# A strided convolution with three products for two outputs, and segments of 25 times instead of 26

## The chip, the cores and the metric

The kernel runs on one core of a Trainium2 chip. The metric is the device time in microseconds (us) of one execution; lower is better. The engines are called by name: TensorE (PE in the profile, its weight loads PEld), VectorE (DVE), ScalarE (ACT), GpSimd (POOL) and SyncE (SP).

## The reference, cut to what matters

An audio tower: seven strided convolutions, each followed by a layer norm over its 128 channels and a GELU, then a projection to 192 features, one attention block and a mixture of nine experts. The change touches the convolutions.

```python
CONVS = [(128, 10, 5)] + [(128, 3, 2)] * 4 + [(128, 2, 2)] * 2    # channels, taps, stride
h = x[:, None, :]                                                # x: 64 rows of 4000 samples
for w, g, b, s in zip(conv_ws, ln_gs, ln_bs, strides):
    h = _conv1d(h, w, s)
    h = jnp.swapaxes(h, -2, -1)
    h = _fp32_layernorm(h, g, b)
    h = jnp.swapaxes(h, -2, -1)
    h = jax.nn.gelu(h, approximate=False)
```

Layer 0 gives 799 times for each row, layer 1 gives 399, then 199, 99, 49, 24 and 12. All is float32.

## The kernel before

The 64 rows are worked in NT = 8 groups of 8. In layers 0 and 1 each row is cut into SEG = 16 segments of LEN1 = 26 layer-1 times, so 8 x 16 = 128 segments lie on the 128 partitions, and the kernel computes 416 layer-1 times for the 399 that are wanted. Layer 0 is computed in LOCALS = 54 local times in blocks of twelve ("quads" q = 0 to 4, the last one shorter), which ScalarE's GELU writes into a ring of four blocks.

The work is written out by hand as a list of slots, SLOTS = HEAD (groups 0 and 1) + BODY for the groups 2 to 6 (16 slots each) + LAST (group 7) + DRAIN. A slot is (chunk, jobs, prep). A chunk (l, g, k) is one PSUM bank of convolution outputs of layer l, group g: up to four blocks of 128 channels for up to 128 positions; CUTS gives the blocks of each chunk. BODY is written relative to g: its slot 0 is (1, g, 0), slot 8 is (1, g, 2), slot 10 is (1, g, 4), slot 11 is (1, g, 3). Each engine walks all slots in the same order and takes its part:

- TensorE: `conv` of slot k's chunk, then `turn` (transposes) of the chunk of slot k - 2, then the jobs, then the token steps (attention and router of a group that is through).
- ScalarE: `square` of slot k, then `gelu` of slot k - 2, then its jobs ("l0": GELU of layer 0).
- VectorE: `norm` of slot k - 1, then `group` (the sum of squares) of slot k, then its jobs ("raw", "z", "xt") and "xs" parts.
- GpSimd: `group` of slot k, a power that turns the sums into factors (L603), then the "pow" parts of layer 0's factors (L597; 12 or 10 columns each), then token steps such as `power_2` (L608 and L610).

So one chunk goes: conv, square (L1378), sum (L1089), power (L603), norm (L1098, which multiplies out of PSUM into `xh`), turn (L771), gelu (L1397). Three PSUM banks hold convolutions, one (`tr`) the transposes, and two hold jobs in turn behind the head: before TensorE starts a job, `room` waits until the job two places ahead of it in the list has been taken out by ScalarE or VectorE.

In layer 1, `conv` multiplies each local time (stationary) with the taps (moving). Outputs j and j + 1 share the local time between them, and so that one is multiplied with two taps at once, 256 columns wide (L751); a chunk of four outputs is 12 blocks of 128 columns. The taps lie in `wt`, W2s holds the experts' second weights, all nine loaded when group 3's samples are.

## Time and profile before

| | us |
|---|---|
| median of 3 runs | 583.17 |
| lowest, highest | 581.24, 583.61 |
| the profiled execution | 581.46 |
| its span, first to last instruction | 579.7 |
| TensorE busy | 549.2 (95%) |
| VectorE, ScalarE, GpSimd busy | 318.1, 316.5, 264.4 |

Busy time is what an engine spent in instructions, and 1.8 us of the profiled execution lie outside its span. float32 products appear as two records each, so "x24" is 12 products. Durations of overlapping instructions of one engine can add up to more than the stretch they fill; the distance between two starts is then the better figure.

### The profile page before, as it was taken

The numbers are of one execution on the slowest core, as the hardware profiler recorded it, in microseconds if no ns is written. First come the engines' busy times: TensorE is split into PE (matmuls) and PEld (weight loads), VectorE is DVE, ScalarE is ACT, GpSimd is POOL, SyncE is SP. The second block draws the span as 40 slices with busy tenths as digits, with TensorE's granted clock in tenths as the row PEclk, the third lists the DMA queues.
The fourth block names the chain that finished last, engine by engine and source line by source line (L and its number), as shares of the span: only waits on it lengthen the run. The fifth ranks groups of instructions, "written<-read, shape, count | busy, mean of one in ns | idle before, by whom it ended". The sixth has DMA issues, their size and how long they took to land.

```text
span 579.7 us, 11208 instructions
## 1 busy us (share of the span) xinstructions
PE 549.2 (95%) x4191; PEld 517.1 (89%) x4191; DVE 318.1 (55%) x751; ACT 316.5 (55%) x499; POOL 264.4 (46%) x297
## 2 busy tenths in 40 slices
PE   6899999999999999999999999999999996899995
PEld 5697999989999999999999989989898975789995
DVE  4666465565567666856574666554654443612231
ACT  1566666747665675558455846574554423344440
POOL 4674394693248426732754294324423030133443
PEclk9999999999999999999999999999999996799999
DMA  6191000792000000000000000000000069051110
GB/s 178 42 329 41 1 1 11 182 211 43 2 1 11 2 6 1 1 7 1 2 0 7 1 1 2 6 1 1 6 2 5 3 174 223 19 158 38 49 38 11
DMA packets 17519, 26.35 MB, mean 45 GB/s; under 512 B 2172, under 2 KB 13397, under 8 KB 17467
## 3 DMA queue, kind: packets, MB, share of 16 engines
q1 hardware_dynamic: 14155, 15.85, 10.1%
q0 software_dynamic: 3296, 9.78, 7.2%
q8 instruction: 35, 0.57, 0.4%
q14 instruction: 17, 0.14, 0.1%
q10 hardware_dynamic: 16, 0.00, 0.0%
HBM read 17.13 MB, written 9.18 MB: 45 GB/s over the span
## 4 chain that ended last, share of the span: by engine, by line
PE 82%; POOL 7%; DVE 4%; ACT 4%; issue 2%; DMA 1%; SPq 1%; POOLq 0%; DVEq 0%; ACTq 0%
PE ps L759 23%; PE ps L751 9%; PE ps L771 7%; PE ps L748 7%; POOL rstd L597 5%; PE ps L1015 4%; PE ps L824 4%; PE ps L1004 3%; PE ps L1003 3%; PE ps L845 3%; PE ps L815 2%; PE ps L886 2%; PE ps L749 2%; PE ps L753 2%; PE ps L906 2%
## 5 line engine op out<-in xcount | busy, mean ns | idle before, releaser
L603 POOL TENSOR_TENSOR rstd<-ssum,neghalf 128x4 f32<-128x4 f32 (+7 forms) x128 | 116.9, 914 | 194.3 <-DVE ssum L1089 194.1
L759 PE MATMUL ps<-wt,wide 128*128 128x128 f32 (+2 forms) x1248 | 151.0, 275 | 4.6 <-ACT wide L1397 4.6
L1378 ACT ACTIVATE work<-ps 128x512 f32<-128x512 f32 (+7 forms) x128 | 67.2, 525 | 161.3 <-PE ps L753 81.9
L759 PEld LDWEIGHTS ps<-wt,wide 128*128 128x128 f32 (+2 forms) x1248 | 144.2, 184 | 7.5 <-issue 6.2
L1089 DVE TENSOR_REDUCE ssum<-work 128x4 f32<-128x516 f32 (+7 forms) x128 | 76.0, 594 | 69.7 <-ACT work L1378 69.2
L1098 DVE TENSOR_TENSOR work<-ps,rstd 128x512 f32<-128x512 f32 (+7 forms) x128 | 76.2, 595 | 68.5 <-POOL rstd L603 67.8
L1397 ACT ACTIVATE wide<-ps,lncol 128x512 f32<-128x512 f32 (+6 forms) x120 | 109.5, 912 | 5.7 <-PE ps L771 5.3
L597 POOL TENSOR_TENSOR rstd<-var,half 128x10 f32<-128x10 f32 (+2 forms) x39 | 82.9, 2133 | 9.0 <-DVE var L1056 8.4
L1408 ACT ACTIVATE h<-ps,lncol 128x512 f32<-128x512 f32 (+1 forms) x120 | 82.0, 730 | 2.4 <-PE ps L824 2.4
L751 PE MATMUL ps<-wt,h 128*128 128x256 f32 x304 | 74.9, 380 | 0.0
L771 PE MATMUL ps<-ident,work 128*128 128x128 f32 (+2 forms) x424 | 66.2, 270 | 0.5 <-DVE work L1098 0.2
L751 PEld LDWEIGHTS ps<-wt,h 128*128 128x128 f32 x304 | 53.5, 191 | 4.9
L748 PE MATMUL ps<-wt,h 128*128 128x128 f32 x416 | 56.0, 276 | 0.2 <-ACT h L1408 0.2
L748 PEld LDWEIGHTS ps<-wt,h 128*128 128x128 f32 x416 | 52.5, 192 | 1.4 <-issue 0.5
L771 PEld LDWEIGHTS ps<-ident,work 128*128 128x128 f32 (+2 forms) x424 | 49.7, 141 | 2.1 <-issue 1.0
L824 PE MATMUL ps<-cols,w0t 120*128 120x512 f32 (+1 forms) x120 | 43.5, 425 | 2.5 <-ACT h L1408 1.6
L1467 ACT ACTIVATE work<-ps 128x768 f32<-128x768 f32 x13 | 10.5, 810 | 35.7 <-PE ps L1004 35.7
L608 POOL TENSOR_TENSOR veps<-mv,eps 96x1 f32<-96x1 f32 x24 | 5.5, 228 | 49.3 <-DVE mv L1108 49.2
L1015 PE MATMUL ps<-W2s,work 128*128 x156 | 27.6, 327 | 0.1
L707 POOL DMA_INDIRECT out_dram<-xnat,idt x13 | 13.1, 1006 | 30.8 <-DVE xnat L1335 30.2
L1077 DVE CAST cols<-ps 120x512 fp32r<-120x512 f32 (+1 forms) x40 | 25.1, 629 | 1.9 <-PE ps L815 1.8
L1318 DVE COPY xst<-ps 96x256 f32<-96x256 f32 x13 | 5.5, 421 | 37.3 <-issue 26.9
(227 smaller groups left out, 833.6 us busy)
## 6 DMA issues: line engine op xcount, KB each, us to landing
sorted_tokens<-zero POOLq DMA_DIRECT2D x1, 5886.5 KB, 33.9
W2s<-in_L_ffn_W_dram SPq DMA_DIRECT2D x9, 576.0 KB, 8.7
wide<-in_L_ffn_W_dram SPq DMA_DIRECT2D x8, 576.0 KB
cols<-sorted_tokens SPq DMA_DIRECT2D x13, 96.5 KB, 2.0
xnat<-in_x_dram SPq DMA_DIRECT2D x7, 135.0 KB
wt<-in_L_ffn_b_dram SPq DMA_DIRECT2D x1, 864.0 KB, 4.4
wide<-in_L_tok_conv_w_dram SPq DMA_DIRECT2D x4, 192.0 KB, 3.4
common_sums<-acc POOLq DMA_DIRECT2D x1, 579.0 KB, 5.3
```

The source lines that it names most:

```text
L597: gp.tensor_tensor(rstd0[:, lo:hi], var0[:, lo:hi], half0[:, lo:hi], ALU.pow).then_inc(s_pow, 1)
L603: gp.tensor_tensor(rstd[0:rows, idx, 0:count], ssum[0:rows, idx, 0:count], neghalf[0:rows, 0:count], ALU.pow).then_inc(rstd_done, 1)
L748: nc.tensor.matmul(y[:, j * C:(j + 1) * C], local(2 * (lo + j) + 1), wt[:, 0, :], start=(j == 0), stop=False)
L751: nc.tensor.matmul(y[:, (j - 1) * C:(j + 1) * C], local(2 * (lo + j)), wt[:, 1:3, :].rearrange("p t c -> p (t c)"), start=False, stop=False)
L759: last = nc.tensor.matmul(y[0:rows, j * C:(j + 1) * C], h[l - 1][g % 2][:, at:at + rows], wt[:, TAP0[l] + tap, :], start=(tap == 0), stop= ...
L771: last = nc.tensor.transpose(tr[:, j * rows:(j + 1) * rows], xh[0:rows, n % 2, j * C:(j + 1) * C], ident[0:rows, 0:rows])
L824: nc.tensor.matmul(o[:, 0:w], w0t[:, j, :], xcol[q % 2][0:12 * K0, 0:w], start=True, stop=True).then_inc(j_done, 1)
L1089: nc.vector.reduce_sum(ssum[0:rows, n % 4, 0:count], sq[0:rows, n % 2, 0:count, :], axis=X).then_inc(ssum_done, 1)
L1098: nc.vector.tensor_tensor(xh[0:rows, n % 2, 0:w].rearrange("p (j c) -> p j c", c=C), ybank(n)[0:rows, 0:w].rearrange("p (j c) -> p j c", c=C),
L1378: nc.scalar.activation(sq[0:rows, n % 2, 0:CUTS[l][k], 0:C], ybank(n)[0:rows, 0:w].rearrange("p (j c) -> p j c", c=C), ACT.Square).then_in ...
L1397: nc.scalar.activation(dst, src, ACT.Gelu, bias=lncol[:, 8 + l:9 + l], scale=lncol[:, l:l + 1]).then_inc(act_done, 1)
L1408: nc.scalar.activation(dst, src, ACT.Gelu, bias=lncol[:, 8:9], scale=lncol[:, 0:1]).then_inc(j_act, 1)
```

## The change

Two outputs of layer 1, y0 = A x0 + B x1 + C x2 and y1 = A x2 + B x3 + C x4, are computed from m = (A + C) x2 as y0 = m + A (x0 - x2) + B x1 and y1 = m + B x3 + C (x4 - x2). For a chunk of four outputs that gives:

- GpSimd makes the four differences with two subtractions of 128x256 (`differences`, prep "df", at the start of a slot's part); it waits for layer 0's ring and for the end of the chunk that last used the buffer. Once, it makes A + C (`wt[:, NTAP]`).
- TensorE does two products for the middle into a job bank (`job_mid`, ahead of the chunk's other products, with `room`'s wait), four with B, waits for the differences, and does four with A or C: ten of 128 columns.
- ScalarE copies the middle out of PSUM (`job_mid`), VectorE adds it to the chunk (`add_mid`) into `ysum` in SBUF, ahead of its `norm` of the slot before; `square` and `norm` read `ysum`. In such slots ScalarE's order is middle, `gelu` of slot k - 2, `square`.
- Segments have 25 times (400 layer-1 times), LOCALS is 51, the last chunk of layer 1 has one output instead of two, layer 0's last quad one triple instead of two, and ROWS_OF shrinks for the layers 2 to 5. As 25 is odd, a layer-1 `gelu` is now two instructions of half the size.
- The new buffers lie in the room of three experts' second weights, which are loaded when the last shared chunk of group 7 is normed instead of at group 3.
- The jobs, "pow" parts and token steps are placed in other slots; LAST keeps its chunks and jobs.

```diff
-LEN1 = 26
-ROWS_OF = [P, P, P, 120, 104, 104, 104]
-LOCALS = 2 * LEN1 + 2
+LEN1 = 25
+ROWS_OF = [P, P, 124, 116, 100, 100, 104]
+LOCALS = 2 * LEN1 + 1
-CUTS = [None, (4, 4, 4, 4, 4, 4, 2), (4, 3, 3, 3), (4, 3), (4,), (2,), (1,)]
+CUTS = [None, (4, 4, 4, 4, 4, 4, 1), (4, 3, 3, 3), (4, 3), (4,), (2,), (1,)]
...
+    ((2, -1, 2), [], []),
+    ((2, -1, 1), [('raw', 1), ('xt', 0, 3)], []),
+    ((2, -1, 0), [], []),
+    ((5, -2, 0), [('l0', 0, 2, 2), ('l0', 0, 3, 0)], []),
+    ((2, -1, 3), [('l0', 0, 3, 2), ('z', 1, 0)], [('pow', 1, 0), ('pow', 1, 1), ('df', 0, 2)]),
+    ((1, 0, 2), [('l0', 0, 3, 1), ('z', 1, 1)], []),
+    ((6, -2, 0), [('xt', 0, 4)], [('pow', 1, 2), ('pow', 1, 3), ('df', 0, 4)]),
+    ((1, 0, 4), [('l0', 0, 4, 0), ('l0', 0, 4, 1), ('l0', 0, 4, 2)], [('pow', 1, 4), ('xs', 1, 0), ('df', 0, 3)]),
+    ((1, 0, 3), [('xt', 1, 0)], []),
+    ((3, -1, 1), [('l0', 1, 0, 1), ('l0', 1, 0, 0)], []),
+    ((3, -1, 0), [('xt', 1, 1), ('l0', 1, 0, 2)], [('df', 0, 5), ('xs', 1, 1)]),
+    ((1, 0, 5), [('l0', 1, 1, 0), ('l0', 1, 1, 1)], []),
+    ((1, 0, 6), [('l0', 1, 1, 2)], [('df', 1, 0)]),
...
+            def differences(g, k):
+                i, lo, count = DIFF[(g, k)], first_block(1, k), CUTS[1][k]
+                quads = range(2 * lo // BLK, 2 * (lo + count) // BLK + 1)
+                gp.wait_ge(j_act, max(ACT_TO[job_at(g, q) + 1] for q in quads))
+                if i >= 2:
+                    gp.wait_ge(conv_done, NUMBER[(1, *DIFFS[i - 2])] + 1)
+                for p in range(count // 2):
+                    at = 2 * lo + 4 * p
+                    before, mid, behind = (local(g, at + d) for d in (0, 2, 4))
+                    out, step = dif[:, i % 2, 2 * p:2 * p + 2, :], behind.offset - before.offset
+                    if step > 0:
+                        ends = bass.AP(before.tensor, before.offset, [before.ap[0], [step, 2], [1, P]])
+                        last = gp.tensor_tensor(out, ends, mid.unsqueeze(1).to_broadcast([P, 2, P]), ALU.subtract)
...
             for k, (chunk, _, prep) in enumerate(SLOTS):
+                for what, g, i in prep:
+                    if what == "df":
+                        differences(g, i)
                 if chunk is not None:
                     group(NUMBER[chunk])
...
+            def job_mid(job):
+                _, g, k = job
+                o = room(job)
+                pe.wait_ge(s_mid, 1)
+                for p in range(CUTS[1][k] // 2):
+                    last = nc.tensor.matmul(o[:, p * C:(p + 1) * C], local(g, 2 * first_block(1, k) + 4 * p + 2), wt[:, NTAP, :],
+                                            start=True, stop=True)
+                last.then_inc(j_done, 1)
...
                 if l == 1:
+                    job_mid(("mid", g, k))
                     for j in range(count):
-                        nc.tensor.matmul(y[:, j * C:(j + 1) * C], local(2 * (lo + j) + 1), wt[:, 0, :], start=(j == 0), stop=False)
-                    nc.tensor.matmul(y[:, 0:C], local(2 * lo), wt[:, 2, :], start=False, stop=False)
-                    for j in range(1, count):
-                        nc.tensor.matmul(y[:, (j - 1) * C:(j + 1) * C], local(2 * (lo + j)),
-                                         wt[:, 1:3, :].rearrange("p t c -> p (t c)"), start=False, stop=False)
-                    nc.tensor.matmul(y[:, (count - 1) * C:count * C], local(2 * (lo + count)), wt[:, 1, :],
-                                     start=False, stop=True).then_inc(conv_done, 1)
+                        nc.tensor.matmul(y[:, j * C:(j + 1) * C], local(g, 2 * (lo + j) + 1), wt[:, 0, :], start=(j == 0), stop=False)
+                    pe.wait_ge(s_diff, DIFF[(g, k)] + 1)
+                    for j in range(count):
+                        last = nc.tensor.matmul(y[:, j * C:(j + 1) * C], dif[:, DIFF[(g, k)] % 2, j, :],
+                                                wt[:, 1 if j % 2 else 2, :], start=False, stop=(j == count - 1))
+                    last.then_inc(conv_done, 1)
...
+            def add_mid(n):
...
+                ve.wait_ge(j_act, ACT_TO[JOB[("mid", g, k)] + 1])
+                ve.wait_ge(conv_done, n + 1)
+                nc.vector.tensor_tensor(made(n)[:, 0:w].rearrange("p (h d c) -> p h d c", h=half, d=2),
+                                        ybank(n)[:, 0:w].rearrange("p (h d c) -> p h d c", h=half, d=2),
...
             for k, (chunk, jobs, _) in enumerate(SLOTS):
-                if chunk is not None:
+                if shares_taps(chunk):
+                    job_mid(NUMBER[chunk])
+                elif chunk is not None:
                     square(NUMBER[chunk])
                 if k >= LAG and ORDER[k - LAG] is not None:
                     gelu(NUMBER[ORDER[k - LAG]])
+                if shares_taps(chunk):
+                    square(NUMBER[chunk])
```

## Rows read from the trace of the kernel before

**Rows 1.** The page: busy time of each engine, shares of the chain that ended last.

```profile
PE 549.2 (95%) x4191; PEld 517.1 (89%) x4191; DVE 318.1 (55%) x751; ACT 316.5 (55%) x499; POOL 264.4 (46%) x297
...
PE 82%; POOL 7%; DVE 4%; ACT 4%; issue 2%; DMA 1%; SPq 1%; POOLq 0%; DVEq 0%; ACTq 0%
```

**Rows 2.** Stretches: length, busy time by engine, granted clock, DMA share, GB/s.

```profile
294.00:348.00 54.00, 53.36 (x431) 50.87 (x430) 34.93 (x79) 33.99 (x55) 27.69 (x28) 1.00 0.01 2
```

**Rows 3.** Chain that ended last, one group: start us, us, what.

```profile
309.57 1.30 PE ps L751 x6
311.47 2.63 PE ps L759 x24
314.10 0.44 PE ps L771 x4
...
319.23 0.46 PE ps L824 x2
...
329.26 0.97 PE ps L906 x12
```

**Rows 4.** TensorE in order of time, one group: start us, us, idle before.

```profile
277.76 0.60 PE L771 MATMUL ps<-ident,work 128*128 128x128 f32 x4
...
283.22 0.66 PE L759 MATMUL ps<-wt,wide 128*104 128x128 f32 x4 [0.63 <-ACT wide L1397]
...
290.54 0.38 PE L753 MATMUL ps<-wt,h 128*128 128x128 f32 x2
...
332.15 0.60 PE L771 MATMUL ps<-ident,work 128*128 128x128 f32 x4
```

**Rows 5.** GpSimd in order of time, same group.

```profile
279.12 0.85 POOL L603 TENSOR_TENSOR rstd<-ssum,neghalf 128x3 f32<-128x3 f32 x1 [2.77 <-DVE ssum L1089]
280.08 4.50 POOL L597 TENSOR_TENSOR rstd<-var,half 128x12 f32<-128x12 f32 x2
...
285.52 1.95 POOL L597 TENSOR_TENSOR rstd<-var,half 128x10 f32<-128x10 f32 x1
287.44 0.55 POOL L603 TENSOR_TENSOR rstd<-ssum,neghalf 104x1 f32<-104x1 f32 x1
287.96 1.96 POOL L597 TENSOR_TENSOR rstd<-var,half 128x10 f32<-128x10 f32 x1
...
290.16 0.84 POOL L610 TENSOR_TENSOR rs<-veps,neghalf 96x1 f32<-96x1 f32 x1
290.97 1.01 POOL L603 TENSOR_TENSOR rstd<-ssum,neghalf 128x4 f32<-128x4 f32 x1
```

**Rows 6.** GpSimd's groups by form: busy us, mean ns.

```profile
L608 POOL TENSOR_TENSOR veps<-mv,eps 96x1 f32<-96x1 f32 x24 | 5.5, 228 | 49.3 <-DVE mv L1108 49.2
...
L573 POOL TENSOR_TENSOR centre<-centre,ident 128x128 f32<-128x128 f32 x1 | 0.5, 453 | 0.1
```

**Rows 7.** ScalarE in order of time, same group.

```profile
311.12 0.60 ACT L1378 ACTIVATE work<-ps 128x512 f32<-128x512 f32 x1 [1.77 <-PE ps L753]
311.62 0.80 ACT L1397 ACTIVATE wide<-ps,lncol 128x256 f32<-128x256 f32 x1
312.20 0.37 ACT L1420 COPY act<-ps 96x192 f32<-96x192 f32 x1
```

**Rows 8.** VectorE in order of time, same group.

```profile
310.36 0.69 DVE L1098 TENSOR_TENSOR work<-ps,rstd 128x512 f32<-128x512 f32 x1 [0.24 <-POOL rstd L603]
```

**Rows 9.** ScalarE's groups by form: busy us, mean ns.

```profile
L1408 ACT ACTIVATE h<-ps,lncol 128x256 f32<-128x256 f32 x24 | 12.4, 556 | 0.0
```

**Rows 10.** Start of the kernel: GpSimd in order of time.

```profile
12.08 10.22 POOL L597 TENSOR_TENSOR rstd<-var,half 128x12 f32<-128x12 f32 x4 [6.49 <-DVE var L1056]
```

**Rows 11.** Start of the kernel: TensorE in order of time.

```profile
21.07 1.05 PE L748 MATMUL ps<-wt,h 128*128 128x128 f32 x8
...
23.70 0.60 PE L815 MATMUL ps<-ident,xhl 128*120 128x128 f32 x4
```

**Rows 12.** DMA issues: KB each, median us to landing.

```profile
W2s<-in_L_ffn_W_dram SPq DMA_DIRECT2D x9, 576.0 KB, 8.7
```

More of the change, by code:

```diff
@@ L150 @@
 LAST = [
-    ((1, 7, 0), [], []),
+    ((1, 7, 0), [], [('df', 7, 1)]),
     ((1, 7, 1), [], []),
@@ L208, with shares_taps @@
 SLOTS = HEAD + [row for g in range(2, NT - 1) for row in body(g)] + LAST + DRAIN
+def shares_taps(chunk):
+    return chunk is not None and chunk[0] == 1 and CUTS[1][chunk[2]] > 1
+SLOTS = [(c, ([("mid", c[1], c[2])] if shares_taps(c) else []) + jobs, prep) for c, jobs, prep in SLOTS]
 AFTER = [('down', 6), ('up', 3, 0), ('up', 3, 1), ('up', 3, 2), ('up', 3, 3), ('up', 3, 4), ('up', 3, 5), ('down', 7)]
@@ L215 @@
 NG = len(CHUNKS)
+FIRST = [n for n, c in enumerate(CHUNKS) if shares_taps(c)]
+PAIRED = {n: i for i, n in enumerate(FIRST)}
+DIFFS = [p[1:] for row in SLOTS for p in row[2] if p[0] == "df"]
+DIFF = {d: i for i, d in enumerate(DIFFS)}
 JOBS = [j for row in SLOTS for j in row[1]] + AFTER
@@ L218 @@
 assert len(JOB) == len(JOBS)
-ON_ACT = ("l0", "up")
-HEAD_JOBS = sum(len(row[1]) for row in HEAD)
+ON_ACT = ("l0", "up", "mid")
+HEAD_JOBS = sum(len(row[1]) for row in SLOTS[:len(HEAD)])
 BANK = [4 + n % 4 if n < HEAD_JOBS else 4 + n % 2 for n in range(len(JOBS))]
@@ L420, in ybank, with made, local @@
             return ps[:, n % 3, :]
+        def made(n):
+            return ysum[:, PAIRED[n] % 2, :] if n in PAIRED else ybank(n)
+        def local(g, at):
+            return ring[:, (QUADS * g + at // BLK) % RING, at % BLK, :]
         def jbank(j):
@@ L597, in power_first @@
                 gp.tensor_tensor(rstd0[:, lo:hi], var0[:, lo:hi], half0[:, lo:hi], ALU.pow).then_inc(s_pow, 1)
+            def differences(g, k):
[11 more added lines that the diff above has]
+                        last = gp.tensor_tensor(out, ends, mid.unsqueeze(1).to_broadcast([P, 2, P]), ALU.subtract)
+                    else:
+                        gp.tensor_tensor(out[:, 0, :], before, mid, ALU.subtract)
+                        last = gp.tensor_tensor(out[:, 1, :], behind, mid, ALU.subtract)
+                last.then_inc(s_diff, 1)
             def group(n):
@@ L975, in _ @@
                 for job in jobs:
-                    if k > 2:
+                    if k > 2 and job[0] != "mid":
                         WORK[job[0]](job)
@@ L1261, in _ @@
                 for job in jobs:
-                    if job[0] not in ON_ACT and k > 2:
+                    if job[0] not in ON_ACT and job[0] != "mid" and k > 2:
                         WORK[job[0]](job)
@@ L1449, in _ @@
                     gelu(NUMBER[ORDER[k - LAG]])
+                if shares_taps(chunk):
+                    square(NUMBER[chunk])
                 for job in jobs:
-                    if job[0] in ON_ACT and k > 2:
+                    if job[0] in ON_ACT and job[0] != "mid" and k > 2:
                         WORK[job[0]](job)
```

132 lines of the change are left out of this document (97 added, 35 removed), and 51 rows, old and new, of tables (BODY, HEAD).

## The prediction

> **What bounds the kernel.** Start with the page [rows 1]: TensorE is busy 95% of the span, and 82% of the chain that ended last runs through it. The stretches say whether that holds in the middle, where the five bodies of 16 slots lie: in one of 54 us TensorE is busy 53.36, VectorE 34.93, ScalarE 33.99, GpSimd 27.69, at the full clock [rows 2]. One body takes 332.15 - 277.76 = 54.39 us, read between two starts of the same transposes, those behind slot 7's convolution [rows 4]. I call that moment E7. So the kernel goes at the rate of TensorE's queue, and every column taken from it is time, as long as what TensorE waits for is there in time. The other engines have 20 to 27 us of air in a body, but they walk in order and in bursts, and that is where this change has to be read.
>
> **What the change takes from TensorE.** The chain gives the pitch: 12 products of 128 columns in 2.63 us, so 0.22 each, and three of 256 in 1.30, so 0.433 each: a wide one is worth two, and time goes by columns [rows 3]. A shared chunk falls from 12 blocks to 10: 2 x 0.22 = 0.43 us. Six of them in a group give 2.6. The chunk with one output instead of two saves three blocks, 0.66, and a transpose, 0.11 (four take 0.44 [rows 3]). Layer 0's last quad is one triple shorter: 3 x 0.06 and one transpose, 0.3 in all; two layer-0 products of 512 columns take 0.46 [rows 3]. The narrower transposes of the layers 2 to 5 give less than 0.1. In all 3.7 us a group, 8 groups, about 29 us: the most that the change can give. Besides, slot 9 waited 0.63 us for the GELU before it in every body [rows 4]; more work now stands between the two, so that this goes: 0.6 more a body. Without any new wait a body would take about 50.1.
>
> **What it adds elsewhere.** On VectorE one add of 512 elements, like the norm at 0.69 [rows 8]: 4.1 a body. On ScalarE a copy out of PSUM, taken as the 128x192 copy at 0.37 [rows 7], and a second instruction for each GELU: a layer-1 GELU of 256 elements lets the next start 0.58 us after it [rows 7], so a pair costs 1.16. On GpSimd two subtractions a chunk. The trace has no such instruction. The two nearest are 228 ns for one column and 453 for 128 [rows 6]; a line through them gives 0.68 us at 256 columns. Bounds: as cheap as the one of 128 columns, 0.45, and twice that, 0.9. Call a chunk's differences D: 1.4 taken, 0.9 to 1.8. All three engines stay below 80% of a body, so none becomes the bound by its sum.
>
> The Trainium skill (GPSIMD Engine Reference, on elementwise work side by side with VectorE) has 4497 ns for an add of 2048 float32 elements and about 2.6 cycles an element at 1.2 GHz, and says to keep such work on VectorE. An estimate from it is 0.56 us and a dispatch for 256 columns; the slope between our two rows, 1.8 ns an element, agrees roughly. By its rate D would be 1.4 to 1.5, and the sum would stay.
>
> **Where it waits: slots 7 to 11.** GpSimd's order there is: power of chunk 7, "pow" 12 and 12 columns, power of chunk 8, differences of chunk (1, g, 4), power of chunk 9, "pow" 10 and 10, `power_2`, differences of chunk (1, g, 3). All of it but the two differences is in today's trace in nearly the same order: it starts at 279.12, which is E7 + 1.36, and ends where the next power starts, at 290.97, with no gap [rows 5]. That is 11.85 us, and with both differences the last of them are there at E7 + 1.36 + 11.85 + 2 x 1.4 = E7 + 16.0. Only then can slot 11 do its last four products, 0.9, and end at E7 + 16.9. Today slot 11's convolution ends at about 290.76 (last products start at 290.54 [rows 4]), E7 + 13.0; nothing on TensorE waited for GpSimd, because the power of a chunk is wanted only two slots later, while differences made in slot 10 are wanted in slot 11. TensorE itself would be there at about E7 + 13.2: three chunks less (-1.3) and the wait of 0.63 gone, but the attention's value products and two layer-0 products moved in (+0.97 and +0.46 [rows 3]), and `out_project` now in the slot of `turn_heads`, behind a ScalarE copy (+0.45; the copy alone is 0.37 [rows 7]). So about 3.7 us of waiting, 2.7 with D at 0.9 and 4.5 at 1.8.
>
> A second wait lies under the first. Slot 10 has three layer-0 jobs and two job banks, so the third needs the first one's GELU, and ScalarE does that behind the pair of GELUs of slot 8's chunk and the square: from the end of its transposes at about E7 + 11.0, plus 1.16, 0.5 (distance between two starts [rows 7]) and 0.4 (a layer-0 GELU of 256 elements takes 0.556 [rows 9], this one has 128). That is E7 + 13.1, where TensorE is at 10.9. The middle of slot 11 needs the next one's GELU too, 13.4. Alone this would let slot 11 end at 13.4 + 2.2 = 15.6.
>
> **The rest of a body.** From the end of slot 11 to the next E7 today: 332.15 - 290.76 = 41.4. Off: three shared chunks 1.3, the short chunk with its transpose 0.8, the value product and layer-0 products that moved 1.4, small things 0.1: 37.8. On: the middle of slot 14 waits for VectorE, which takes the xt job out only behind the sum of slot 13's squares, 0.5; in slot 15 and slot 0 a job waits for the GELU of the job two places ahead, 0.15 and 0.4. That is 38.9. A body: 16.9 + 38.9 = 55.8, against 54.4, or **+1.4**, five times +7.
>
> **Head, group 1, end.** In the head GpSimd is full until 22.3 [rows 10], then makes A + C (0.45, as the 128x128 row [rows 6]) and the first differences, so that the first chunk ends near 25.1 where today it ended by 23.70 [rows 11]: +1.4. After that, GpSimd has six differences, five powers of the factors and seven chunk powers, about 24 us, where TensorE's queue of these chunks took about 25: what the columns give is taken by waits, and I carry +1. Group 1 has its differences ahead of the long powers: -4.3 and 1.6 of job waits, -2.7. Group 7 has no "pow" parts: -3.7, with 0.5 of waits and a chain longer by the add, 0.8, where the last chunks drain: -2.4. The late weights cost nothing: three loads at 8.7 us each [rows 12], even one behind the other 26 us, with the whole drain as cover; without it they would be on the path.
>
> **The sum.** +7 + 1 - 2.7 - 2.4 = +2.9 on the profiled execution's 581.46: 584.4. The median of the runs is 1.7 above that execution, so 586.1; the drain's order is the part I trust least and more likely loses than gains, so I say **587**.
>
> **Rivals.** (a) No wait at all beside small job waits: bodies at 51.5, five times -2.9; head -3.5, group 1 -2.7, end -2.4: 558.4, as a median **560**. For it speaks the air on every engine [rows 2]; against it the GpSimd queue, which needs 14.1 + 2D where 13.2 is free: it decides even at D = 0. Chance 0.08. (b) The subtractions are at the low end or partly hidden and ScalarE's pair is cheap: bodies at about 54, -0.4 each: -2 and 0 - 2.7 - 2.4, that is -7, **576**. Chance 0.17. (c) Bodies break even at 54.4 to 55: 579 to 583, "within 0.5%" together with the low part of my own case. (d) D at 1.8 and longer, because VectorE's and GpSimd's accesses disturb each other: bodies 56.7, +2.3 each, head +3: 594, as a median **596**; the trace has no case for or against. Chance 0.12. My own case, waits in slots 10 and 11 of each body that eat the gain: 0.63, of which about half lies below 586.
>
> **Range and chances.** A measurement here tells 0.5% from no change, 2.9 us. My case alone runs from 580 to 592, by D from 0.9 to 1.8 (+-0.9 a body) and the head (+-2). With (b) and most of (d) in: 573 to 596. Faster by over 0.5% (below 580.3): (a), (b) and a little: 0.27. Slower (above 586.1): half of my case and (d): 0.45. Between: 0.28.
>
> **What would show it.** Right: TensorE waits for GpSimd's subtraction in front of the last products of (1, g, 3), 3 to 4 us in each of five bodies; a body, measured E7 to E7, of 55 to 56.5; a pitch of 2.2 us for a shared chunk; TensorE busy about 520. GpSimd without a gap from the power of slot 7 to the subtractions of slot 10. Wrong: subtractions near 0.3 us, or an order on GpSimd in which they pass the "pow" parts; bodies near 51 with the waits gone. If the wait before slot 11 is there but names ScalarE, the job banks were the bound and not GpSimd.

## The result

| | before | changed |
|---|---|---|
| median of the runs, us (4 each, the two kernels in turn) | 583.39 | 607.93 |
| lowest, highest | 581.24, 585.61 | 607.1, 609.0 |
| span of the profiled execution | 579.7 | 606.7 |
| mean granted clock in it | 0.984 | 0.979 |

The ratio is 1.0421, 95% interval 1.0377 to 1.0466. I had said 587.0, range 573 to 596: the sign is right, the size is not, and the time lies outside the range.

The page of the changed kernel, against [rows 1]:

```profile
PE 540.1 (89%) x4239; PEld 504.0 (83%) x4239; DVE 367.9 (61%) x803; ACT 340.0 (56%) x603; POOL 335.7 (55%) x402
...
PE 59%; POOL 18%; DVE 10%; issue 6%; ACT 5%; DMA 0%; SPq 0%; POOLq 0%; DVEq 0%; ACTq 0%
...
L644 POOL TENSOR_TENSOR W2s<-h 128x256 f32<-128x256 f32 x88 | 69.1, 804 | 5.8 <-ACT h L1520 5.7
...
L1188 DVE TENSOR_TENSOR work<-W2s,rstd 128x512 f32<-128x512 f32 x48 | 39.6, 825 | 21.8 <-POOL rstd L654 21.1
```

The chain shows it at once: TensorE's share of what ended last fell from 82% to 59%, GpSimd's rose from 7% to 18%. TensorE is busy 9 us less and the span is 27 us longer, so its idle time went from 30.5 to 66.6 us. Stretches of the changed kernel, columns as in [rows 2]:

```profile
0.00:60.00 60.00, 46.80 (x301) 42.37 (x302) 37.72 (x87) 31.65 (x55) 43.51 (x57) 0.94 0.40 113
...
300.00:360.00 60.00, 54.02 (x449) 50.31 (x448) 44.27 (x89) 38.52 (x71) 38.95 (x44) 1.00 0.01 3
```

In the middle TensorE is busy 90%, where it was 99% [rows 2]; VectorE and GpSimd now have about 15 to 21 us in 60 without work, and they had 19 to 26 in 54.

**Where the 27 us come from.** I read the start of slot 9's four products of 104 positions, the one with the 0.63 wait of [rows 4], in each group from 2 to 7: before 119.90 to 391.18, after 126.82 to 416.58. Head and group 1: +6.9. Five bodies: 289.76 against 271.28, +18.5 (56.8, 58.3, 58.0, 58.1, 58.5, where one took 54.3). From there to the end: +1.6.

**One body.** TensorE in order of time, changed kernel; the first and the last row are the moments E7 of one body and the next:

```profile
294.25 0.59 PE L848 MATMUL ps<-ident,work 124*128 124x124 f32 x4
...
308.22 0.33 PE L900 MATMUL ps<-cols,w0t 120*128 120x128 f32 x1 [2.06 <-ACT h L1520]
...
308.77 0.68 PE L790 MATMUL ps<-wt,h 128*128 128x128 f32 x4 [0.22 <-ACT h L1520]
309.29 1.06 PE L819 MATMUL ps<-wt,h 128*128 128x128 f32 x8
311.15 1.16 PE L822 MATMUL ps<-wt,W2s 128*128 128x128 f32 x8 [0.80 <-POOL W2s L644]
312.14 0.25 PE L848 MATMUL ps<-ident,work 104*128 104x104 f32 x1
...
321.12 0.68 PE L790 MATMUL ps<-wt,h 128*128 128x128 f32 x4 [0.67 <-DVE cols L1154]
...
326.67 0.68 PE L790 MATMUL ps<-wt,h 128*128 128x128 f32 x4 [0.37 <-ACT h L1520]
...
328.79 1.16 PE L822 MATMUL ps<-wt,W2s 128*128 128x128 f32 x8 [0.54 <-POOL W2s L644]
...
352.38 0.59 PE L848 MATMUL ps<-ident,work 124*128 124x124 f32 x4
```

L790 is the middle, L819 the products with B, L822 those with the differences. The body takes 58.13. The third layer-0 job of slot 10 waits for ScalarE (L900, 2.06), and slot 11's last products wait for GpSimd (L822, 0.80). A label counts from the modelled end of the product before. By starts, L819 to L822 takes 1.86 where an unbroken chunk takes 0.89, so the wait labelled 0.80 costs 0.97. Eight waits of the body carry a label, 5.4 us in all; by starts there are eleven, about 7.5 us. Two bodies earlier the same two waits have another outcome:

```profile
191.79 0.47 PE L900 MATMUL ps<-cols,w0t 120*128 120x128 f32 x1 [2.06 <-ACT h L1520]
...
193.32 1.91 PE L819 MATMUL ps<-wt,h 128*128 128x128 f32 x8
```

The eight records with B take 1.91 us instead of 1.06, and the mean granted clock of that body is 0.97, where it is 1.00 in the other four.

GpSimd in the stretch of the body shown first, against [rows 5]:

```profile
301.36 1.01 POOL L654 TENSOR_TENSOR rstd<-ssum,neghalf 128x4 f32<-128x4 f32 x1 [0.20 <-DVE ssum L1166]
302.33 0.46 POOL L646 TENSOR_TENSOR W2s<-h 128x128 f32<-128x128 f32 x1
302.75 0.91 POOL L647 TENSOR_TENSOR W2s<-h 128x128 f32<-128x128 f32 x1
303.62 0.72 POOL L644 TENSOR_TENSOR W2s<-h 128x256 f32<-128x256 f32 x1
304.30 0.55 POOL L654 TENSOR_TENSOR rstd<-ssum,neghalf 104x1 f32<-104x1 f32 x1
304.82 3.88 POOL L630 TENSOR_TENSOR rstd<-var,half 128x10 f32<-128x10 f32 x2
...
309.69 1.40 POOL L644 TENSOR_TENSOR W2s<-h 128x256 f32<-128x256 f32 x2
...
326.88 1.86 POOL L644 TENSOR_TENSOR W2s<-h 128x256 f32<-128x256 f32 x2
```

The last differences are there at 311.09, which is E7 + 16.8 (I had said + 16.0). The ring wraps inside chunk (1, g, 4): its differences take three instructions and 1.97 us, from 302.33 to 304.30, instead of 1.4. And two of these rows are too long for their kind: L647 with 0.91 beside L646 with 0.46, and the pair at 326.88 with 1.86. VectorE in the same stretch:

```profile
302.40 0.94 DVE L1188 TENSOR_TENSOR work<-W2s,rstd 128x512 f32<-128x512 f32 x1
...
309.34 2.27 DVE L1147 TENSOR_TENSOR xhl<-xsc,xhl 128x480 fp32r<-128x480 f32 x1
...
326.94 1.21 DVE L1188 TENSOR_TENSOR work<-W2s,rstd 128x512 f32<-128x512 f32 x1 [0.68 <-POOL rstd L654]
```

These have both operands in SBUF and run beside GpSimd's subtractions; the same multiply (L1188) takes 0.69 elsewhere in the body, that for `xhl` 0.67 in the kernel before (mean of 7). GpSimd's pair at 309.69 is not longer for it, but the power behind the pair, which starts at 311.06 while the multiply still runs, takes 1.43 us instead of 1.01.

**The head.** TensorE in order of time, changed kernel:

```profile
35.87 0.27 PE L891 MATMUL ps<-ident,xhl 128*120 128x128 f32 x1
38.90 0.88 PE L900 MATMUL ps<-cols,w0t 120*128 120x128 f32 x3 [2.76 <-DVE cols L1154]
...
40.53 1.91 PE L819 MATMUL ps<-wt,h 128*128 128x128 f32 x8
42.23 1.92 PE L822 MATMUL ps<-wt,W2s 128*128 128x128 f32 x8
...
45.37 1.06 PE L819 MATMUL ps<-wt,h 128*128 128x128 f32 x8
```

One wait of 2.76 us, and behind it the same eight records take 1.91 instead of 1.06: the engine runs at the lower of its two levels, 1.2 GHz, for 5 to 6 us. The stretch to 60 has a granted clock of 0.94. The wait alone doesn't decide that: in `df_early` below, whose head is the same, TensorE waits the same 2.76 us, the eight records behind take 1.06, the stretch to 60 has a clock of 1.00, and slot 9 of group 2 starts at 124.45 instead of 126.82.

### The profile page after: what moved, and what is told of

Same layout as the page of the kernel before. It is cut to its first block, busy times and chain, and to the rows that moved or that the text cites. A ratio compares the mean times of both kernels' runs of the same rounds, so it can differ in the third digit from the quotient of the medians.

```text
span 606.7 us, 11753 instructions
## 1 busy us (share of the span) xinstructions
PE 540.1 (89%) x4239; PEld 504.0 (83%) x4239; DVE 367.9 (61%) x803; ACT 340.0 (56%) x603; POOL 335.7 (55%) x402
## 4 chain that ended last, share of the span: by engine, by line
PE 59%; POOL 18%; DVE 10%; issue 6%; ACT 5%; DMA 0%; SPq 0%; POOLq 0%; DVEq 0%; ACTq 0%
PE ps L829 19%; POOL rstd L630 6%; POOL W2s L644 5%; PE ps L822 5%; POOL rstd L654 4%; PE ps L848 4%; PE ps L1091 4%; PE ps L1080 3%; PE ps L1079 3%; PE ps L921 3%; PE ps L819 2%; DVE ssum L1166 2%; ACT work L1478 2%; PE ps L900 2%; PE ps L962 2%
## 5 line engine op out<-in xcount | busy, mean ns | idle before, releaser
L654 POOL TENSOR_TENSOR rstd<-ssum,neghalf 128x4 f32<-128x4 f32 (+8 forms) x128 | 117.0, 914 | 160.8 <-DVE ssum L1166 160.3
L829 PE MATMUL ps<-wt,wide 128*124 128x128 f32 (+3 forms) x1248 | 149.3, 274 | 1.9 <-ACT wide L1509 1.7
L829 PEld LDWEIGHTS ps<-wt,wide 128*124 128x124 f32 (+3 forms) x1248 | 142.8, 180 | 4.8 <-issue 3.0
L1166 DVE TENSOR_REDUCE ssum<-work 128x4 f32<-128x516 f32 (+8 forms) x128 | 75.0, 586 | 46.5 <-ACT work L1478 44.7
L1495 ACT ACTIVATE wide<-ps,lncol 128x256 f32<-128x256 f32 (+1 forms) x112 | 74.3, 771 | 37.7 <-PE ps L848 37.7
L630 POOL TENSOR_TENSOR rstd<-var,half 128x12 f32<-128x12 f32 (+3 forms) x39 | 78.9, 2035 | 6.0 <-DVE var L1133 6.0
L644 POOL TENSOR_TENSOR W2s<-h 128x256 f32<-128x256 f32 x88 | 69.1, 804 | 5.8 <-ACT h L1520 5.7
L848 PE MATMUL ps<-ident,work 128*128 128x128 f32 (+3 forms) x416 | 65.7, 271 | 3.8 <-DVE work L1188 3.5
L822 PE MATMUL ps<-wt,W2s 128*128 128x128 f32 x384 | 53.6, 283 | 9.2 <-POOL W2s L644 9.1
L900 PE MATMUL ps<-cols,w0t 120*128 120x512 f32 (+1 forms) x120 | 43.8, 424 | 17.9 <-ACT h L1520 13.2
L822 PEld LDWEIGHTS ps<-wt,W2s 128*128 128x128 f32 x384 | 47.7, 195 | 12.3 <-POOL W2s L644 12.0
L1188 DVE TENSOR_TENSOR work<-ps,rstd 124x384 f32<-124x384 f32 (+7 forms) x80 | 41.9, 523 | 22.2 <-POOL rstd L654 21.5
L1188 DVE TENSOR_TENSOR work<-W2s,rstd 128x512 f32<-128x512 f32 x48 | 39.6, 825 | 21.8 <-POOL rstd L654 21.1
L819 PE MATMUL ps<-wt,h 128*128 128x128 f32 x384 | 52.4, 281 | 0.0
L819 PEld LDWEIGHTS ps<-wt,h 128*128 128x128 f32 x384 | 48.4, 198 | 0.0
L790 PE MATMUL ps<-wt,h 128*128 128x128 f32 x192 | 32.2, 292 | 8.3 <-ACT h L1520 4.0
L900 PEld LDWEIGHTS ps<-cols,w0t 120*128 120x128 f32 x120 | 20.3, 193 | 21.7 <-ACT h L1520 16.3
```

Source lines behind the costliest of these rows:

```text
L630: gp.tensor_tensor(rstd0[:, lo:hi], var0[:, lo:hi], half0[:, lo:hi], ALU.pow).then_inc(s_pow, 1)
L644: last = gp.tensor_tensor(out, ends, mid.unsqueeze(1).to_broadcast([P, 2, P]), ALU.subtract)
L654: gp.tensor_tensor(rstd[0:rows, idx, 0:count], ssum[0:rows, idx, 0:count], neghalf[0:rows, 0:count], ALU.pow).then_inc(rstd_done, 1)
L819: nc.tensor.matmul(y[:, j * C:(j + 1) * C], local(g, 2 * (lo + j) + 1), wt[:, 0, :], start=(j == 0), stop=False)
L822: last = nc.tensor.matmul(y[:, j * C:(j + 1) * C], dif[:, DIFF[(g, k)] % 2, j, :], wt[:, 1 if j % 2 else 2, :], start=False, stop=(j == co ...
L829: last = nc.tensor.matmul(y[0:rows, j * C:(j + 1) * C], h[l - 1][g % 2][:, at:at + rows], wt[:, TAP0[l] + tap, :], start=(tap == 0), stop= ...
```

## The experiments

All ratios are to the kernel before, run beside it on the same chip. My theories then: (1) the waits in slots 10 and 11 and their like stand one behind the other on TensorE, so that taking them away in order gives the columns back; (2) the added work loads VectorE, ScalarE and GpSimd so tightly in order that a wait taken away only comes back elsewhere. The rival was that not the sharing, but the new slots or the clock, cost the time.

### Which part costs

`seg25_old_slots`: only the segments of 25; layer 1 as before, old slots.

```diff
-def shares_taps(chunk): return chunk is not None and chunk[0] == 1 and CUTS[1][chunk[2]] > 1
+def shares_taps(chunk): return False      # and conv's products, BODY, HEAD, LAST of the kernel before
```

> Segments of 25 times alone, with the three taps as before and the slots of before. By columns it saves 1.07 us a group (three blocks, one transpose, the shorter last quad), 8.6 us: 575 if nothing on the other engines matters. If the second GELU instruction, which an odd 25 needs, is what hurts (ScalarE's queue as the cause), 583 or more.

577.5 us, ratio 0.9919 (0.9893 to 0.9945). Half of the change is worth 0.8%. The columns that it takes from a body come to about 1.1 us by the prediction's prices, and 0.4 arrives: the five bodies take 269.33 us instead of 271.28. I put the rest down to the two GELUs of half the size, which take 823 ns each where one took 1178; no run separates that. The wait for them in slot 9 stays:

```profile
PE ps L831 <- ACT wide L1511: 4.8, 7, 0.9
```

(TensorE's waits: what waits for what, us in total, times, longest.)

`no_sharing_new_slots`: segments of 25 and the new slots, without the "df" parts; layer 1 as before.

> The slots and segments of the change, but three taps for each output as before: no middle, no differences, no add. Theory 1 (what the shared products add on GpSimd, ScalarE and VectorE, and where it queues, costs the time): near the run with the old slots, 575 to 582. Theory 2 (the new placement of jobs and token steps costs it by itself): 590 or more. Theory 1 expects the third layer-0 job of slot 10 still to wait about 2 us a body, as that is a matter of the job banks, so that this run is some 5 to 8 us above the one with the old slots.

585.75 us, ratio 1.0064 (1.0041 to 1.0087). A body takes 55.1.

`sharing_old_slots`: the whole change, but BODY and HEAD as before, with "df" added to their prep, for example:

```diff
-    ((1, 0, 2), [('xt', 0, 4)], [('pow', 1, 2)]),
-    ((6, -2, 0), [('l0', 0, 4, 0), ('l0', 0, 4, 1)], [('pow', 1, 3)]),
+    ((1, 0, 2), [('xt', 0, 4)], [('pow', 1, 2), ('df', 0, 4)]),
+    ((6, -2, 0), [('l0', 0, 4, 0), ('l0', 0, 4, 1)], [('pow', 1, 3), ('df', 0, 3)]),
```

> The shared products in the slots and token places of before, with the differences put ahead of the long powers. With three taps the new slots cost 8 us over the old ones. If sharing pays once the slots are good: 560 to 570, below the 577.5 of segments of 25 alone. If the job of the middle and the longer chain cost more than the columns give in any of these orders: 585 to 600, above both 577.5 and 582.3.

639.88 us, ratio 1.0972 (1.093 to 1.1015); neither theory had that. TensorE's waits:

```profile
PE ps L822 <- POOL W2s L644: 20.7, 15, 3.7
PE ps L790 <- ACT h L1520: 9.7, 12, 2.0
PE ps L891 <- DVE xhl L1147: 8.9, 6, 1.7
```

So the parts come apart. Segments -0.8%; the new slots +1.5% for a kernel that doesn't share; the sharing +3.5% on the new slots and +10.6% on the old (ratios divided: 1.0421 / 1.0064 and 1.0972 / 0.9919). The new slots help the kernel that shares and hurt the one that doesn't. Against `no_sharing_new_slots`, by the same marks as above, the changed kernel loses 7.0 us up to slot 9 of group 2 (126.82 against 119.84), 15.6 in the five bodies (289.76 against 274.19) and 0.1 behind them.

### Take the GpSimd wait away

`df_early`: the differences of chunk (1, g, 3) a slot earlier.

```diff
-    ((6, -2, 0), [('xt', 0, 4)], [('pow', 1, 2), ('pow', 1, 3), ('df', 0, 4)]),
-    ((1, 0, 4), ..., [('pow', 1, 4), ('xs', 1, 0), ('df', 0, 3)]),
+    ((6, -2, 0), [('xt', 0, 4)], [('pow', 1, 2), ('pow', 1, 3), ('df', 0, 4), ('df', 0, 3)]),
+    ((1, 0, 4), ..., [('pow', 1, 4), ('xs', 1, 0)]),
```

> The changed kernel with the differences of (1, g, 3) made one slot earlier, ahead of the two long powers. The 0.8 us labelled wait (0.96 by starts) in front of the last products of (1, g, 3) goes in each of five bodies. If GpSimd's queue is what costs the time: 15 us or more faster, below 593. If the job banks and ScalarE are right behind it, as the rows say: 4 to 5 us faster, 603.

607.68 us, ratio 1.0448 (1.0423 to 1.0473). The wait in slot 11 is gone, and next to nothing is gained in time:

```profile
PE ps L900 <- ACT h L1520: 13.2, 9, 2.1
PE ps L822 <- POOL W2s L644: 7.2, 11, 1.3
```

The job bank's wait (L900) has its 13.2 us as in the changed kernel. The bodies say where the gain went. The one body with a clock of 1.00 takes 57.02 us, 1.0 to 1.1 less than the changed kernel's (58.01 and 58.11), about what the wait had cost (0.97). The other four have a mean clock of 0.97 and take 58.2 to 59.1; the changed kernel has one such body. The runs agree: the mean clock of all four is 0.973 to 0.976 here and 0.979 to 0.984 there.

`df_early_jobs_spread`: also layer 0's jobs spread, no more than two to a slot between slots 8 and 15.

> As the run before, and the three layer-0 jobs of slot 10 moved behind slots 11 and 12, the jobs of layer 0 after them each one slot later. If the job bank's wait (2.3 us by starts) and the one behind it (0.44) are the other half of the loss, a body gets 3.7 us shorter against the change, 0.96 of them from the differences: five bodies, 18 us, 590. If the waits only move to the next job that needs a bank: 600 to 603.

634.47 us, ratio 1.0901 (1.0857 to 1.0946). L900's wait fell to 3.7, but three others took its place, and bodies take 60 to 65, all five below full clock (0.92 to 0.97):

```profile
PE ps L790 <- ACT h L1520: 17.3, 12, 2.1
PE ps L891 <- DVE xhl L1147: 8.7, 6, 1.8
PE ps L790 <- DVE work L1188: 5.8, 5, 1.2
```

### One job for the last quad

Layer 0's last quad has one triple, so its three jobs of 128 columns fit into one bank. `one_job_quad` does them as one job with one GELU.

```diff
+                if q == QUADS - 1:
+                    for i in range(3):
+                        last = nc.tensor.matmul(o[:, i * P:(i + 1) * P], w0t[:, i, :], xcol[...][0:12 * K0, 0:P], start=True, stop=True)
+                    last.then_inc(j_done, 1)
+                    return
```

> The changed kernel, and layer 0's last quad (three products of 128 columns) as one job: one bank, one GELU of 384 elements instead of three of 128. The third job's wait of slot 10 (2.3 us by starts) goes. If waits stand behind one another, as theory 1 says, GpSimd's differences of (1, g, 3) come at the same time as before and slot 11 ends where it did: 603 to 607. If the job banks alone were the bound: 12 us faster, 596 or less.

618.38 us (612.67 to 621.3), ratio 1.0599 (1.0522 to 1.0675). Neither forecast has that. The job-bank wait is gone and what stood behind it is seen. TensorE in order of time:

```profile
309.85 1.06 PE L820 MATMUL ps<-wt,h 128*128 128x128 f32 x8
314.44 2.07 PE L823 MATMUL ps<-wt,W2s 128*128 128x128 f32 x8 [3.53 <-POOL W2s L645]
```

and the stretch in which it lies:

```profile
300.00:360.00 60.00, 54.17 (x431) 51.24 (x430) 42.29 (x83) 35.84 (x66) 36.37 (x42) 0.94 0.01 3
```

The wait for GpSimd is 3.53, not 0.80, and the four products behind it take 2.07 instead of 1.16. Four short waits in a row (0.40, 2.06, 0.22, 0.80) had left the clock at 1.00 in the body of the changed kernel shown above; the one long one costs about as much waiting, and the lower clock on top. The products start 11.26 us behind slot 9's (303.18), in the changed kernel 11.22 (299.93), as theory (1) says. All five bodies are below full clock here, and take 58.5 to 61.1.

`one_job_quad_df_early` adds the edit of `df_early`.

> The same, with the differences of (1, g, 3) made a slot earlier. Now both waits of slots 10 and 11 are gone and theory 1 expects their sum, 3.7 us a body, five bodies: 586 to 591. If the waits only move on into other slots (theory 2: too much work on the three engines in any order): 600 or more.

606.93 us, ratio 1.0402 (1.0357 to 1.0447). Two bodies keep a clock of 1.00 and take 55.5 and 56.7; the other three take 58.3 to 58.7. Slot 11 now runs without a wait, and the next thing is late:

```profile
306.00 0.25 PE L849 MATMUL ps<-ident,work 104*128 104x104 f32 x1
307.79 0.63 PE L892 MATMUL ps<-ident,xhl 128*120 128x128 f32 x4 [1.53 <-DVE xhl L1154]
308.93 0.29 PE L934 MATMUL ps<-ident,xn 96*96 96x96 f32 x1 [0.51 <-DVE xn L1209]
...
309.13 3.81 PE L830 MATMUL ps<-wt,wide 128*116 128x128 f32 x18
```

(18 records take 2.13 elsewhere.)

`quad_df_behind_group`: the same, with those differences behind slot 9's chunk power on GpSimd instead of ahead of it.

> One job for the last quad, and the differences of (1, g, 3) in slot 9 behind that slot's chunk power instead of ahead of it. In the run with them ahead, TensorE then stood 1.53 us for the xt job's samples (VectorE's xs part in slot 10) and lost another 1.7 us to the half clock behind that wait. If the norm behind a late chunk power delayed the xs part: 3 to 12 us faster than 606.9. If the xs part is late because it stands behind slot 10's sum of squares: no change, 604 to 608.

606.24 us, ratio 1.0395 (1.035 to 1.044). The wait for `xhl` stays (7.3 us in all, 6 times), so the differences weren't what made it late.

`quad_df_behind_group_xs`: "xs" (VectorE's scaled samples, `xhl`) a slot earlier as well.

> The same, with the xs part moved from slot 10 to slot 9, ahead of slot 10's wait for its sum of squares. Theory 1 expects the 1.53 us wait to go and with it the clock's fall behind it, 3.7 us a body in all, less a new wait for norm_2 (0.5): 588 to 594, still above 577.5, since 3 us a body of small waits and the head stay. If waits always find another place: 600 or more.

610.16 us (606.24 to 614.84), ratio 1.0493 (1.0436 to 1.055). The wait for `xhl` has gone, and:

```profile
PE ps L852 <- DVE work L1198: 5.5, 8, 1.4
PE ps L937 <- DVE xn L1212: 5.2, 6, 1.6
PE ps L895 <- ACT h L1533: 4.5, 9, 0.7
```

`seg25_one_job_quad`: one job for the last quad, without sharing, old slots.

> Segments of 25 with the old slots and three taps, with one job for the last quad: no wait there to remove, TensorE's work the same, ScalarE 0.7 us less a group. 575 to 578, that is the same as the run without it within 0.5%.

577.63 us, ratio 0.9915 (0.9882 to 0.9949): no different from `seg25_old_slots`.

### Make GpSimd's subtractions small

These three subtract one column for each local time instead of 128, so the convolution's outputs are not the reference's; all else is done.

```diff
-last = gp.tensor_tensor(out, ends, mid.unsqueeze(1).to_broadcast([P, 2, P]), ALU.subtract)
+last = gp.tensor_tensor(out[:, :, 0:1], ends[:, :, 0:1], mid.unsqueeze(1).to_broadcast([P, 2, P])[:, :, 0:1], ALU.subtract)
```

`small_differences` (the changed kernel):

> The changed kernel with each subtraction cut to one column of each local time (two columns an instruction), so that its output is not the reference's: GpSimd's instructions, waits and order stay, only about 0.5 us of each is gone. If GpSimd's time for the differences is what costs most of the 24 us: 590 or less. If ScalarE and the job banks wait behind it, as moving the differences hints at (it took the wait away and not the time): 598 to 605.

600.08 us (596.85 to 603.84), ratio 1.0301 (1.0236 to 1.0365). A subtraction takes 259 ns, and the 13.2 us of L900's wait for ScalarE stay.

`one_job_quad_small_df`:

> One job for the last quad, and the subtractions cut to one column (output not the reference's). Against the run with small differences alone (600.1) theory 1 expects 2.7 us a body, 13 us: 586. Theory 2: 598 or more. It also says what GpSimd's time costs once the job wait is gone.

587.8 us (585.76 to 593.15), ratio 1.0104 (1.0035 to 1.0172). Bodies take 55.06. TensorE's waits, and a stretch:

```profile
PE ps L824 <- POOL W2s L646: 7.2, 5, 1.5
```
```profile
300.00:360.00 60.00, 56.19 (x479) 53.16 (x477) 42.44 (x97) 40.46 (x74) 31.99 (x45) 1.00 0.01 3
```

`quad_df_group_xs_small` (the edits of `quad_df_behind_group_xs`):

> The same with the subtractions cut to one column (output not the reference's): what the shared products could give in this order if GpSimd's elementwise time were nothing. 575 to 583 if GpSimd's time is the main cost; near the run before it if it is not.

589.42 us, ratio 1.0113 (1.0076 to 1.015); bodies 54.8. That is above its forecast of 575 to 583.

The pair `one_job_quad` and `one_job_quad_small_df` differs in the size of GpSimd's subtractions alone, and by 30 us. GpSimd is busy 335.2 and 282.3 us, but VectorE too falls from 370.1 to 346.1, with the same instructions: `norm` out of SBUF from 825 to 690 ns, `xhl`'s multiply from 1657 to 660. Their spans are 615.8 and 586.1, their mean clocks 0.965 and 0.984. A mean of m over two levels, full and half, means that 2 (1 - m) of the span is at half speed, and half of that is lost: 21.6 and 9.4 us. So some 12 of the 30 are clock, if TensorE was at work in that time, and the rest is waiting. By the same sum the changed kernel lost 12.7 and the one before 9.3: of its 27 us some 3.4 are clock.

### VectorE's order

`norm_first`: in VectorE's loop `norm` of the slot before goes ahead of `add_mid`.

```diff
-                if shares_taps(chunk):
-                    add_mid(NUMBER[chunk])
                 if k >= 1 and ORDER[k - 1] is not None:
                     norm(NUMBER[ORDER[k - 1]])
+                if shares_taps(chunk):
+                    add_mid(NUMBER[chunk])
```

> The changed kernel with VectorE's norm of the slot before ahead of the add of this slot, so that the norm no longer stands behind the wait for this slot's convolution. If the norm's lateness holds TensorE's transposes: 3 to 8 us faster, 600 to 605. If nothing waits for it, because the transposes come only behind the next convolution: 606 to 609.

622.79 us, ratio 1.0676 (1.0642 to 1.071): slower by 15 us than the changed kernel, which I had not expected. The first 60 us show the larger part of it:

```profile
0.00:60.00 60.00, 44.37 (x263) 39.96 (x264) 34.94 (x83) 30.32 (x51) 41.96 (x55) 0.91 0.40 113
```

The mean clock is 0.963 and the wait in the head grew from 2.76 to 3.7. `norm` waits for GpSimd's power, and everything behind it on VectorE, the add of the middle first, waits along. Up to slot 9 of group 2 this kernel loses 8.1 us to the changed one (134.90 against 126.82), in the five bodies 3.8, of which three instead of one are at 0.97. With the old slots as well:

> The same swap on the shared products in the old slots. The old slots have fewer job-bank waits, so the norm chain may show more: within 1 us of the run without the swap if the job banks bound both, 3 us or more faster if the chain does.

655.09 us, ratio 1.1235 (1.1197 to 1.1274).

### The sum in PSUM instead of SBUF

In the pair of runs above VectorE got faster when GpSimd's subtractions got small: part of their price may be that the two engines hinder each other. `sum_in_psum` writes the sum with the middle back into the chunk's PSUM bank, which `square` and `norm` read as in the kernel before.

```diff
-            return ysum[:, PAIRED[n] % 2, :] if n in PAIRED else ybank(n)
+            return ybank(n)
...
-                if n - 3 in PAIRED:
-                    pe.wait_ge(s_whole, PAIRED[n - 3] + 1)
-                elif n >= 3:
+                if n >= 3:
                     pe.wait_ge(xh_done, n - 2)
```

> The changed kernel with the sum of chunk and middle written back into its PSUM bank instead of SBUF, so that square and norm read PSUM as in the kernel before. Theory P: in the changed kernel VectorE's multiplies with both operands in SBUF and GpSimd's subtractions delay each other: norm out of SBUF took 825 ns on average with the subtractions of full size and 690 with small ones, and the worst norm took 1.21 us beside a pair of subtractions of 1.86 instead of 1.40. With the operand in PSUM norm goes back to 0.69 everywhere and GpSimd's pair in slot 0 to 1.4, which shortens the wait of slot 0's last products by about 0.5 us: bodies 57.0 to 57.8 instead of 58.1, the kernel at 602 to 606. The multiply for xhl (1.66 us for 128x480, mean) stays long. Rival S: 825 is simply the price of two SBUF operands and independent of GpSimd; then norm goes to 0.69 too, but the subtractions stay at a mean of 804 ns, and the time stays at 606 to 609. Against both: a PSUM bank is now released by norm and not by the add, some 2 us later, and TensorE may wait for a bank: then 608 to 614.

606.89 us (605.88 to 611.96), ratio 1.0422 (1.0358 to 1.0487). `norm` takes 689 ns, the subtraction's mean is 741 instead of 804, and TensorE's waits for the differences fall from 9.1 us in 13 to

```profile
PE ps L820 <- POOL W2s L644: 2.9, 6, 0.8
```

No time is gained from it: 602 to 606 was the forecast of theory P, whose durations came. The clock is 0.967, not 0.979. TensorE in slots 10 and 11 of the body shown above:

```profile
305.23 0.33 PE L898 MATMUL ps<-cols,w0t 120*128 120x128 f32 x1 [2.07 <-ACT h L1518]
305.77 1.11 PE L790 MATMUL ps<-wt,h 128*128 128x128 f32 x4 [0.22 <-ACT h L1518]
306.67 1.91 PE L817 MATMUL ps<-wt,h 128*128 128x128 f32 x8
```

The waits ahead of them are those of the changed kernel to 0.01 us, but here the clock falls behind them and in that body it didn't. Four of the five bodies are at 0.97 here (57.7 to 58.3 us; the fifth takes 55.9), one in the changed kernel. By the sum above, 20.0 us of this span are lost to the clock, 7.3 more than in the changed kernel, against 6.2 us of waits for GpSimd that went.

`quad_df_early_psum` has the same edit in `one_job_quad_df_early`.

> One job for the last quad, the differences of (1, g, 3) a slot earlier, and the sum in PSUM. Without the sum in PSUM it ran at 606.93. Theory P: only the multiply for xhl (128x480, 740 ns there) still has both operands in SBUF, and norm falls from 826 to 690 ns: 600 to 605, with the waits for xhl and xn in slot 12 some tenths shorter. Rival: those waits are set by the order of VectorE's queue, with the squares of slot 10 ahead, and not by its durations: 606 to 609.

600.78 us (598.77 to 602.01), ratio 1.0287 (1.0239 to 1.0334), where it was 606.93 with the sum in SBUF: 1.0% less, with the clock at 0.970 and 0.973. No wait for the differences is among TensorE's longest seven any more (7.5 us in 11 before); the wait for `xhl` in slot 12 is what it was (7.4). This is the best version that shares with whole subtractions.

**Bodies at the same clock.** In each profiled execution I take the five bodies, from one slot 9 to the next, and leave out the first and the last, which border on other parts. Those with a granted clock of 1.00 can be compared without the clock:

| | bodies at 1.00 among the middle three, us | of all five, below 1.00 |
|---|---|---|
| before | 54.7, 54.6, 54.4 | 0 |
| `seg25_old_slots` | 54.2, 54.1, 54.2 | 0 |
| `no_sharing_new_slots` | 55.1, 55.1, 55.1 | 0 |
| changed | 58.0, 58.1 | 1 |
| `df_early` | 57.0 | 4 |
| `one_job_quad_df_early` | 56.7 | 3 |
| `quad_df_behind_group` | 56.8, 56.7 | 2 |
| `small_differences` | 56.0 | 4 |
| `quad_df_early_psum` | 55.9 | 3 |
| `one_job_quad_small_df` | 55.1, 55.1, 55.1 | 0 |

Within one kernel a body at 0.97 takes 1.2 to 1.7 us longer than one at 1.00 (58.33 and 57.02 in `df_early`, 58.41 and 56.68 in `quad_df_behind_group`). `one_job_quad` and `sum_in_psum` have no middle body at 1.00.

## Why the prediction had the sign and missed the size

- **What bounds it; the columns.** Right as far as TensorE's own work goes: an unbroken shared chunk takes 2.23 us (28.37 to 30.60 in the head), 2.2 said. Wrong in what follows: "TensorE busy about 520" came out at 540.1. Behind a wait the same records take longer (1.16 instead of 1.06, 0.68 instead of 0.61), so that eleven waits a body stand in the busy time as well as in the idle time; where the clock falls, busy time grows by all that is at half speed.
- **The body, the first step that failed: +1.4 said, +3.7 measured,** 18.5 instead of 7 over five. E7 to the end of slot 11 is 17.9 (16.9 said), the rest 40.2 (38.9 said). The joint wait in slots 10 and 11 is right in size: 3.9 by starts (0.16, 2.3, 0.44 and 0.97), 3.7 said. By the names on the labels, my own test, most of it is ScalarE's and the job banks' (2.06 and 0.22 against 0.80). What ended last was GpSimd all the same: slot 11's last products start at 311.15, 0.06 behind the differences, and `one_job_quad`, without ScalarE's waits, starts them no earlier. So slot 11 ends late because the differences come at E7 + 16.8 and not + 16.0, and 0.57 of that is slot 9: its differences take 1.97 for 1.4, for the wrap, which `step > 0` in the diff announces, and for the multiply beside them. In the rest of the body I had waits of 1.05, and by starts they are about 2.25: slot 14's middle 0.77 (0.5 said), slot 15's job 0.23 (0.15), slot 0's middle 0.54 (0.4), and slot 0's differences 0.71, for which I had nothing.
- **D.** 1.4 taken, 1.4 measured for a pair that runs undisturbed (1.40 at 309.69). But a pair beside a multiply with both operands in SBUF takes 1.86, and that multiply 1.21 instead of 0.69. I had written of this that the trace had no case for or against, and did not see that the change itself moves `norm`'s operand from PSUM to SBUF. The Trainium skill has the rule (SBUF — State Buffer, on who interferes with whom): a VectorE instruction with two SBUF inputs contends with a GpSimd instruction that reads SBUF. The runs agree: 825 ns beside full subtractions, 690 beside small ones, 689 out of PSUM. `quad_df_early_psum`, without `norm`'s part of it, ran 6 us shorter than the same with it, 0.8 in a body at full clock (56.7 to 55.9); in the changed kernel's own order (`sum_in_psum`) no time came of it.
- **Head and group 1, the second step: -1.7 said, +6.9 measured.** The first chunk ended near 24.5 (25.1 said). What I hadn't followed is VectorE: the copy of the samples for layer 0's last quad comes behind `add_mid`, `norm` and a sum of squares that itself waits 0.89 us for ScalarE. TensorE waits 2.76 us for it and then runs at half clock for 5 to 6 us. With the same head at full clock (`df_early`) 4.5 of the 6.9 stay. Group 1's -2.7 never arrived.
- **End, the third: -2.4 said, +1.6 measured.** Against `no_sharing_new_slots` the part behind the bodies costs nothing and gains nothing, so here too what the columns give is waited away; which wait does it I did not separate. Against the kernel before, all of it lies in the first 38.4 us behind that mark (36.6 before); from there the two are level (151.7 and 151.9). No wait of TensorE names the late weights; their loads took 6.9 us each (8.7 in [rows 12]).
- **The clock was no term.** The trace before shows 1.00 in every stretch up to 480, and I carried that over to a kernel with waits in every slot. By the sum above it costs the changed kernel 3.4 us more than the one before, and the variants up to 17 (`df_early_jobs_spread`).
- **Rivals.** (a) and (b) fall with the traces. (d) had the right mechanism, VectorE and GpSimd disturbing each other, but its D of 1.8 holds for one pair in a body only. The rest of the loss is many small waits together, for which I had no case.
- **Sums that don't come out.** TensorE's terms up to slot 11 add up to E7 + 12.95, not 13.2, which makes the joint wait 3.9. Rival (d) with the end and group 1 of my own sum gives 592.6 as a median, not 596. And the air in [rows 2] is 19 to 26 us, not 20 to 27. None of these reaches the 20 us that were missed.

Of the two theories each holds in part. Where only GpSimd's wait was taken away (`df_early`), it came back nowhere: a body at full clock got shorter by 1.0 to 1.1 us. Taking away the job banks' 2.7 on top brought 0.3, because 1.53 and 0.51 appeared in slot 12: that is theory (2). And much of what the bodies gained the clock took back, at 1.2 to 1.7 us for each body in which it fell. The medians alone (606.2 to 634.5 for seven re-orderings of the shared kernel on the new slots) look like theory (2) only. Why the clock falls in four bodies of `df_early` and in one of the changed kernel, the runs do not show. What brought more was a shorter time in VectorE and GpSimd: 600.8 with the sum in PSUM, 587.8 with small subtractions. The last has bodies of 55.1, as `no_sharing_new_slots` has, which still waits for the job banks (10.4 us in 9 waits for layer 0's GELU): even with GpSimd's elements nearly free and that wait gone the columns give nothing. The new slots with one job for the last quad and without sharing, its fair rival, were not run. Open remain: what moves the clock in the head, which is at 0.94 in `seg25_old_slots` too, with nothing shared, though there between 10 and 30 us; why `norm_first` loses so much there, beyond the reading above; and whether another order of ScalarE's GELUs would have helped, which was not tried. The best version is `seg25_old_slots`, level with `seg25_one_job_quad`: 577.5 us, below both kernels.

## What to carry to other kernels

A column taken from a nearly full TensorE is worth its price only where every engine that must now deliver earlier has slack in its own order at that slot; a busy share of 55% says nothing of it. Where a change puts an operand of VectorE from PSUM into SBUF and gives GpSimd elementwise work at the same time, price the two beside each other. Compare variants stretch by stretch at the same granted clock before saying that a wait came back elsewhere: a body of `df_early` was 1 us shorter, and the median did not show it. And time the parts of a change one by one: here a part that gives 0.8% was hidden under two that cost 5%.
